# Attention, two deformable blocks and a bottleneck on one core: short loops with staged index slots in the gather stages, weighting in PSUM and corner sums on TensorE, column and row strips in two products

## The reference

```python
out = gather(y0, x0) * (wy0 * wx0)[:, None] + gather(y0, x0 + 1) * (wy0 * wx1)[:, None] \
    + gather(y0 + 1, x0) * (wy1 * wx0)[:, None] + gather(y0 + 1, x0 + 1) * (wy1 * wx1)[:, None]
...
out = jnp.einsum('bckhw,ock->bohw', samp, w2.reshape(w2.shape[0], w2.shape[1], 9))
```

## Time and profile before

| | |
|---|---|
| median of 3 runs | 6745.91 us (6744.83 to 6750.26) |
| the profiled execution | 6749.49 us |
| its span | 6747.7 us |
| TensorE busy | 5426.3 us, 80% |
| DVE busy | 4983.7 us, 74% |
| ACT busy | 3474.2 us, 51% |
| POOL busy | 2026.8 us, 30% |
| mean granted TensorE clock | 0.889 |

### The profile page before, as it was taken

The page is one execution under the profiler, slowest core; times in us unless marked ns, Lnnn a source line. Parts: engine busy times, 40 slices in busy tenths (PEclk is TensorE's granted clock), DMA queues, the critical chain, the costliest instruction groups (busy, mean ns, idle before and its releaser), DMA issues. The chain is left out here.

```text
span 6747.7 us, 126038 instructions
## 1 busy us (share of the span) xinstructions
PE 5426.3 (80%) x38156; PEld 3715.8 (55%) x38156; DVE 4983.7 (74%) x12163; ACT 3474.2 (51%) x6593; POOL 2026.8 (30%) x2338
## 2 busy tenths in 40 slices
PE   5999989998533679878869999899984336798798
PEld 3777757776322444454437777577753225444544
DVE  4999979996333479759959998799953334797698
ACT  3888868885100135425538887688841001354254
POOL 0000000000377247427600000000003772573275
PEclk9999999999655789989989999999996557899899
DMA  2000000000222379759910000000002224797699
GB/s 66 3 3 3 3 21 3 4 3 28 63 82 82 115 277 409 288 194 410 379 48 3 3 3 3 21 3 4 3 27 67 82 82 121 288 409 271 212 410 361
DMA packets 369615, 819.33 MB, mean 121 GB/s; under 512 B 109347, under 2 KB 196710, under 8 KB 368387
## 3 DMA queue, kind: packets, MB, share of 16 engines
q0 software_dynamic: 193536, 679.59, 26.4%
q1 hardware_dynamic: 175874, 137.17, 7.3%
HBM read 709.75 MB, written 94.26 MB: 119 GB/s over the span
## 5 line engine op out<-in xcount | busy, mean ns | idle before, releaser
L1476 DVE TENSOR_SCALAR_CACHE_REDUCE arena<-ps 128x512 f32<-128x512 f32 x2048 | 1395.5, 682 | 89.4 <-DVEq L1475 87.3
L1496 DVE TENSOR_TENSOR arena<-ps,arena 128x512 f16<-128x512 f32 x2048 | 1405.3, 687 | 32.4 <-DVEq L1495 21.9
L637 POOL DMA_INDIRECT arena<-corners,arena x1152 | 1092.9, 949 | 984.7 <-POOLq L628 597.4
L767 PEld LDWEIGHTS ps<-arena 128*128 128x128 f16 x16384 | 1057.0, 98 | 553.3 <-issue 242.0
L1031 ACT ACTIVATE arena<-arena 128x1024 f32<-128x1024 f32 x1024 | 1175.6, 1148 | 324.0 <-ACTq L1029 324.0
L1038 ACT ACTIVATE arena<-ps 128x512 f16<-128x512 f32 x2048 | 1187.6, 592 | 234.8 <-ACTq L1037 219.9
L752 PE MATMUL ps<-arena 128*128 128x512 f16 x4096 | 1224.3, 381 | 85.1 <-PEq L750 81.8
L767 PE MATMUL ps<-arena 128*128 x16384 | 1248.9, 219 | 14.2 <-PEq L763 12.8
L781 PE MATMUL ps<-ident_s,arena 128*128 128x128 f32 x8192 | 1244.4, 274 | 0.3 <-issue 0.3
L1165 ACT ACTIVATE ps<-arena 128x256 f32<-128x256 f32 x1152 | 549.0, 478 | 1015.7 <-DMA arena<-corners,arena 985.0
L946 PE MATMUL ps<-arena 128*128 128x512 f32 x2304 | 1054.3, 601 | 0.0
(11 more groups left out here) (131 smaller groups left out, 4291.6 us busy)
## 6 DMA issues: line engine op xcount, KB each, us to landing
corners<-arena SPq DMA_DIRECT2D x256, 256.0 KB, 3.9
arena<-corners,arena POOLq DMA_INDIRECT x1728, 8.8
arena<-arena SPq DMA_DIRECT2D x192, 64.0 KB, 1.9
arena<-in_wd SPq DMA_DIRECT2D x4, 2304.0 KB, 8.2
X<-in_x SPq DMA_DIRECT2D x2, 4096.0 KB, 12.4
attn_scratch<-arena SPq DMA_DIRECT2D x256, 32.0 KB, 1.5
arena<-attn_scratch SPq DMA_DIRECT2D x16, 512.0 KB
corners<-arena SPq DMA_DIRECT2D x128, 64.0 KB, 2.2
```

What stands on the lines that cost most here:

```text
L637: pool.indirect_dma_start(G3[slot].rearrange("p a c -> p (a c)"), None, table256, bass.IndirectOffsetOnAxis(ap=IDX3[:, 4 * g + t, k:k + 1] ...
L767: last = mm(ps[:, 6 + p, 0:2 * D], part[:, g % 4, k * 128:(k + 1) * 128], V[:, bass.ds(j * NHEAD + 2 * pair + h, 1), :, :].rearrange("p o ...
L1476: v.tensor_scalar(S[p][:, g * CHUNK:(g + 1) * CHUNK], ps[:, g % 2, :], float(D) ** -0.5 / QK_SCALE ** 2, -3.0e38, ALU.mult, ALU.max, accum ...
L1496: v.tensor_tensor(P2[:, g % 4, :], ps[:, 2 + g % 4, :], P1[:, g % 4, :], ALU.subtract).then_inc(p2_ready, 1)
```

## The change

Six things change together.

1. In the 64-channel gather stage ACT, not POOL, copies the nine indices, four tiles ahead, into four slots (IS2). DVE copies the weights to PSUM and makes one product into PR2, with the corners as outermost dimension; SP hands `weighted` on as `pr_ready` (to TensorE) and `g2_free` (to POOL). The two additions go: TensorE sums the four corners and transposes at once, with 4 accumulating products with the identity for each of five column blocks. ACT copies the sums in two instructions.
2. TensorE sums tile t + 1 ahead of the products of tile t; at the end one round of sums works on a buffer that nobody reads.
3. The 256-channel gather stages become loops: three taps a turn on POOL, ACT and DVE, nine on TensorE, one half a turn on SP. Weights and indices lie in the order of the steps, and ACT copies them to short buffers (WS3, IS3) for each step. Semaphores are counted down as they are used; SP passes `half_done` on as `acc_free`, `samp_ready` and `g_free`. G3 has 12 slots, SAMP and ST have three buffers, the outputs one pair of PSUM banks. One semaphore counts a half's two gathers.
4. The 256-to-64 product makes two chunks at once, one in each 64-column strip of the array; ACT reads them from their own partitions, with the coefficients copied there once (bnf1).
5. In the projection the position rows of the two outputs lie in two row strips (POSL is loaded twice), all after both main products, and both outputs are announced together.
6. `corners` writes indices and weights in the order of the steps and has a buffer of its own for the floors.

```diff
-                with pool.Fori(0, NT // 2) as t2:
-                    for p in range(2):
-
+                with pool.Fori(0, NT // 4) as t4:
+                    for q in range(4):
+                        p = q % 2
+                        pool.wait_ge(is_ready, 1)
+                        pool.sem_inc(is_ready, -1)
                         pool.wait_ge(g2_free, 1)
                         pool.sem_inc(g2_free, -1)
-                        pool.tensor_copy(IS2[p], IDX2[:, bass.ds(2 * t2 + p, 1), :]
-                                                                 .rearrange("p a k -> p (a k)")).then_inc(pool_step, 1)
-                        pool.wait_ge(pool_step, 1)
-                        pool.sem_inc(pool_step, -1)
                         for k in range(KK):
                             pool.indirect_dma_start(G2[p][:, k, :], None, table64,
-                                                        bass.IndirectOffsetOnAxis(ap=IS2[p][:, k:k + 1], axis=0)).then_inc(g2_ready[p], 16)
+                                                    bass.IndirectOffsetOnAxis(ap=IS2[:, q, k:k + 1], axis=0)).then_inc(g2_ready[p], 16)
...
-                    corner4 = G2[p].rearrange("p k (q c) -> p (k q) c", q=4)
-                    v.tensor_tensor(corner4, corner4, WS2[p].unsqueeze(2).to_broadcast([128, KK * 4, CB]),
-                                         ALU.mult).then_inc(dve_step, 1)
-                    dve.wait_ge(dve_step, 1)
-                    dve.sem_inc(dve_step, -1)
-                    v.tensor_tensor(A2, G2[p][:, :, 0:2 * CB], G2[p][:, :, 2 * CB:4 * CB], ALU.add).then_inc(dve_step, 1)
...
-                    v.tensor_tensor(SM2[p][:, 0:KK * CB].rearrange("p (k c) -> p k c", k=KK),
-                                        A2[:, :, 0:CB], A2[:, :, CB:2 * CB], ALU.add).then_inc(sm_ready, 1)
+                    v.tensor_tensor(PR2[p].rearrange("p q (k c) -> p k q c", k=KK),
+                                    G2[p].rearrange("p k (q c) -> p k q c", q=4),
+                                    w.rearrange("p (k q) -> p k q", q=4).unsqueeze(3).to_broadcast([128, KK, 4, CB]),
+                                    ALU.mult).then_inc(weighted, 1)
...
+                def summed(p):
+
+                    pe.wait_ge(pr_ready, 1)
+                    pe.sem_inc(pr_ready, -1)
+                    for i in range(5):
+                        rows = 128 if i < 4 else CB
+                        for q in range(4):
+                            last = mm(ps[0:rows, 6 * p + i // 4, (i % 4) * 128:(i % 4 + 1) * 128],
+                                      PR2[p][:, q, i * 128:i * 128 + rows], ident_s[:, :],
+                                      start=(q == 0), stop=(q == 3))
+                    last.then_inc(smt_ps, 1)
...
+                summed(0)
                 with pe.Fori(0, NT // 2) as t2:
                     for p in range(2):
...
+                        summed(1 - p)
+                        mixed(p)
...
+                def staged2(t, q):
+
+                    p = q % 2
+
+                    act.wait_ge(smt_ps, 1)
+                    act.sem_inc(smt_ps, -1)
+                    act.sem_inc(pr_free, 1)
+                    af(SMT2[p][:, 0:4, :].rearrange("p a b -> p (a b)"), ps[:, 6 * p, :],
+                       ACT.Copy).then_inc(smt_ready, 1)
+                    af(SMT2[p][0:CB, 4, :], ps[0:CB, 6 * p + 1, 0:128], ACT.Copy).then_inc(smt_ready, 1)
+                    af(IS2[:, q, :], IDX2[:, bass.ds(t + 4, 1), :].rearrange("p a k -> p (a k)"), ACT.Copy).then_inc(is_ready, 1)
...
+                    def samples_done():
+
+                        sp.wait_ge(half_done, 1)
+                        sp.sem_inc(half_done, -1)
+                        sp.sem_inc(acc_free, 1)
+                        sp.sem_inc(samp_ready, 1)
+                        sp.sem_inc(g_free, 2)
...
-                    for g in range(NCH):
-                        for k in range(KK):
+                    with pool.Fori(0, TAPS // 3) as i:
+                        for k in range(3):
+                            pool.wait_ge(is_ready, 1)
+                            pool.sem_inc(is_ready, -1)
                             for t in range(4):
-
-                                j = g * KK + k
-                                slot = 4 * (j % 4) + t
-                                if j >= 4:
-                                    pool.wait_ge(samp_ready, 4 * (j - 4) + t + 1)
+                                if t % 2 == 0:
+                                    pool.wait_ge(g_free, 2)
+                                    pool.sem_inc(g_free, -2)
...
+                    def products(i, k):
+
+                        act.wait_ge(act_step, 1)
+                        act.sem_inc(act_step, -1)
+                        for h in range(2):
+                            act.wait_ge(acc_free, 1)
+                            act.sem_inc(acc_free, -1)
+                            act.wait_ge(g_ready[k][h], (i + 1 + (2 * b + layer) * (TAPS // 3)) * 32)
+                            act.sem_inc(gathers_seen, 1)
+                            for t in (2 * h, 2 * h + 1):
+                                af(ps[:, h, (t % 2) * C:(t % 2 + 1) * C], G3[4 * k + t][:, 0, :], ACT.Copy,
+                                       scale=WS3[:, k, 4 * t:4 * t + 1]).then_inc(prod_ready, 1)
+                        weights(3 * i + k + 1, (k + 1) % 3)
+                        af(IS3[:, k, :], IDX3[:, bass.ds((3 * i + k + 3) * 4, 4)], ACT.Copy).then_inc(is_ready, 1)
...
                     transposes(0)
-                    for j in range(1, KK * NCH):
-                        pe.wait_ge(st_ready, CH)
-                        pe.sem_inc(st_ready, -CH)
-                        transposes(j)
-                        tap(j - 1)
-                    pe.wait_ge(st_ready, CH)
-                    pe.sem_inc(st_ready, -CH)
-                    tap(KK * NCH - 1)
+                    with pe.Fori(0, NCH) as g:
+                        for k in range(KK):
+                            pe.wait_ge(st_ready, CH)
+                            pe.sem_inc(st_ready, -CH)
+                            transposes((k + 1) % 3)
+                            tap(k)
...
                     for half in range(CH):
-                        last = mm(ps[0:CB, 0, :], w1_s[:, half, :], X[:, half, chunk(n)],
-                                  start=(half == 0), stop=(half == CH - 1))
-                    last.then_inc(h1_ready, 1)
+                        for q in range(2):
+                            last = mm(ps[q * CB:(q + 1) * CB, 0, :], w1_s[:, half, :], X[:, half, chunk(n + q)],
+                                      start=(half == 0), stop=(half == CH - 1), tile_position=(0, q * CB))
+                    last.then_inc(h1_ready, 2)
...
-                            for k in range(2):
-                                last = mm(ps[:, 2 + oh, k * C:(k + 1) * C], POSL[p][:, k, oh * 128:(oh + 1) * 128],
-                                          pos_r_s[:, :], start=False, stop=(k == 1))
-                            last.then_inc(proj_ready, 1)
+                        for k in range(2):
+                            for oh in range(CH):
+                                group = slice(32 * oh, 32 * oh + 6)
+                                last = mm(ps[:, 2 + oh, k * C:(k + 1) * C], POSL[p][group, k, oh * 128:(oh + 1) * 128],
+                                          pos_r_s[group, :], start=False, stop=(k == 1), tile_position=(32 * oh, 0))
+                        last.then_inc(proj_ready, 2)
```

387 lines of the change are left out of this document (228 added, 159 removed).

## The result

The changed kernel takes 6547.6 us (median of 4 runs, 6541.42 to 6553.52); the kernel before takes 6745.37 beside it (4 runs, 6742.45 to 6750.26). The ratio is 0.9706, with a 95% interval from 0.9689 to 0.9723: 198 us less, where 151 were forecast.

The account below looks back on a forecast made before the run. POOL's issuing was taken to bound the 64-channel stage, transfers the 256-channel stages. Terms -170 + 16 + 0 + 3 = -151 against 6749.5 gave 6598, stated as 6594 us because that execution was 3.6 above the median; range 6550 to 6690.

Parts of the forecast that it names:

- Term 1: 64-channel gather stage: gathers 1.2525 us apart, -94.6 us a batch, less a longer end of +10; -85 a batch, -170.
- rival A: 64-channel stage: TensorE stays at the lower clock and bounds it at 12.9 us a tile; 6701 us; chance 0.16.
- Term 2: Four 256-channel gather stages: transfers keep the pace, new hand-overs and loops add +4 us a layer, +16.
- The transfers set the pace: 256-channel stages: a tap of four gathers takes 5.13 us at 409 GB/s, unchanged in bytes and operations.
- The parts that I named as not hidden: 256-channel stages: 0.5 us for the first index copy, 2.0 for the last tap's relay, wait and dummy transposes.
- The 1.5 at the group boundaries: 256-channel stages: outputs 0.6 us later at seven group boundaries, about two thirds absorbed by DVE's margin; 1.5 us a layer.
- Rival C: 256-channel stages: relayed hand-overs become the pace; at 0.7 us a tap on top of the forecast, 6796; chance 0.06.
- The ring of 12: 256-channel stages: 12 gather slots instead of 16 leave 4 us and more of queue and cost nothing.
- Term 3: Projection: paired position rows save, later announcement and longer TensorE pause cost; the two nearly cancel, 0 taken.
- Both bounds: Projection: net between -1.06 and +0.72 us a chunk, -17 to +12 us over 16 chunks.
- Term 4: 256-to-64 product: SP's table writes set the pace, only the first pair of chunks can cost; +1.5 a batch, +3.
- The lower bound: 256-to-64 product: 0 us a batch if the strips overlap (first pair 3.65 us), against +3.6 if they don't.

Follow-up runs that it names:

- Three runs: Changed kernel with POOL copying the nine indices: 6596.01 us; changed kernel with the product's weights in SBUF: 6647.36; kernel before with those weights in PSUM: 6669.77.
- six of the variants: Changed kernel with the 256-channel loops written out on ACT alone (7257.32, 7254.93, 7262.92 us) or DVE alone (7256.18, 7225.01, 7239.98).

## Why the prediction was right or wrong

**Term 1, the 64-channel stage: right, in sum and in its parts.** Forecast -85 a batch, measured -84.3 and -84.9. From the first to the last gather 359.5 us were forecast and 358.9 are there. Three runs gave the prices one by one: the copy 0.73 us a tile, the second SBUF source 1.5 (437.5 - 388.2 over 32 tiles), and in the kernel before 1.2 for the product alone with the rest passing to the addition. TensorE's clock came out at 0.79 and a tile of TensorE at some 9 to 10 us, both inside what I gave; rival A needed 0.50. The end took 24.2 us from the last gather to the last update, 26 forecast; what I had not counted is POOL's drain, 3.5 us a batch. A slip that changed nothing: TensorE's products behind the sums take 4.53 us by the earlier trace rows, where I wrote 4.3.

**Term 2, the 256-channel stages: wrong in sign, and the failing step is "The transfers set the pace: ... 5.13 us a tap".** I took the steady tap and the mean rate of the stage's middle for the pace. The mean tap was 5.250 us in the first such stage, since every eighth tap waited 1 us more for one DMA engine, and after the change 5.148. (In the last stage it was 5.355 and is 5.255; there every ninth tap is long in both kernels, 6.86 and 7.6 us, at the group boundaries, where DVE takes the outputs out of PSUM.) I knew that the change turned written-out code into loops, and counted what loops add on DVE (2.4 us) but nothing for what the fetching of code costs: it is 25 us, in four stages. The parts that I named as not hidden were right in their sum: 0.5 at the start and 2.0 at the end forecast, 0.97 and 1.42 measured, 2.4 together. The 1.5 at the group boundaries are not to be seen, for DVE makes them up at 4.70 us a tap. With all loops written out, that is with the hand-overs alone, the stages are 1.3, 2.0, 2.7 and 1.7 us longer than before: +7.7 where I had +16. Rival C did not come near: the taps stay at 5.12. The ring of 12 was nothing, as forecast.

**Term 3, the projection: -11.4 where I took 0.** Both bounds held and the middle did not. The position rows: 1.06 us a chunk less, the whole of what I had as the most, 0.86 by the strips and 0.20 by the order. TensorE's pause: 1.58 instead of 1.04 to 1.14, +0.44 to 0.54, where I had 0.7. A third part I had not seen: the main product of both outputs takes 3.60 us from start to start where it was 1.88 and 1.91, -0.19. That makes -0.71 to -0.81, and the chunk went from 8.05 to 8.14 us to 7.34. Eight such chunks are 6 us a stage; measured are 3.7 in the first batch and 7.7 in the second, and the difference goes with the clock: the second projection of the kernel before stood at 0.50 for its first 18 us and took 79.6 us, the first took 75.1. The drain at a change of tiling mode, by the Trainium skill (TensorEngine Tiling (Array Packing), Key Properties), does not appear as time: the position rows start at 1638.53, 0.07 before the modelled end of the product in front of them, and the transposes 1.06 after that.

**Term 4, the 256-to-64 product: -0.9 where I took +3.** The lower bound held: the strips overlap in full. That SP's table writes set the rest was right; the edit bought nothing.

**The sum.** Missed by 34 us in term 2, 11 in term 3 and 4 in term 4. The range's low end came from the bounds of the terms, and term 2's lower bound of 0 had left out the gain that came. The last 2.4 us beyond the range are less than the runs of the changed kernel differ by (6541.42 to 6553.52), so on which side of 6550 the median fell is chance; that term 2 had the wrong sign is not.

## What to carry to other kernels

Where a stage waits for every transfer to land, its pace is that of the slowest DMA engine, and the mean share and the GB/s don't show it: look at the taps one by one, and count the instruction packets beside the transfers. A loop in place of some thousand written-out instructions each on ACT and DVE was worth up to 2% of such a stage here, more than the relays that it needed cost. And an instruction with two SBUF sources on DVE stops the gathers that POOL issues inside it for the rest of its time: one source in PSUM frees them, but only if the next such instruction goes as well.

## What was not expected of the hardware

- One fetch of 8 KB of DVE's code took 0.34 us and slowed the next two data packets from 0.16 to 0.50 and 0.48 us; at each the last of a gather's 16 landings fell another 0.8 to 1.0 us back, up to 9.1 us behind the first in the kernel before. Fetches of 16 KB for TensorE cost a stage of 390 us only 1 to 2 us for all ten.
- Two column strips overlap fully even when the second chunk's products stand behind all of the first chunk's in the program: 3.69 and 3.68 us, at the lower clock.
- POOL's drain at the end of the 64-channel stage takes 5.93 or 5.94 us in both batch elements of five kernels. In the kernel before it starts while gathers still run, and ends 5.95 and 5.94 us behind the last of them.
- The table stage of the same code takes from 68 to 78 us, and the two traces looked at differ in the clock that the second half gets. In the changed kernel its second half ran at 0.68, in the kernel with all loops written out at 0.50 (second row):

```profile
1726.00:1763.00 37.00, 29.77 (x116) 19.01 (x116) 16.34 (x43) 2.90 (x5) 0.00 (x0) 0.68 0.35 66
```

```profile
1729.00:1773.00 44.00, 40.21 (x121) 25.14 (x119) 16.36 (x43) 2.94 (x5) 0.00 (x0) 0.50 0.30 56
```

- Beside six of the variants the kernel before took 500 us more, and those variants of the changed kernel took as long as it did: a whole gain can go, and in the traces it goes with instructions that TensorE and ACT start late, and not with the gathered data.
